# Local attention with values behind scores, and a feed-forward that reads its shifted input by copies and multiplies in three rounded passes

## The chip, the core and the metric

One NeuronCore of a Trainium2 chip runs the whole program. The metric is the device time of that one core, in microseconds (us). The kernel before was timed three times: 2302.34, 2305.26 and 2305.34 us, a median of 2305.26 us.

## What is computed

The input x has 16 batches of 128 tokens by 128 features, all float32. Four steps follow, each with a residual: a cross attention of 16 heads of 8, a mixture of 16 experts (6 per token), a cross attention of 8 heads of 64 with rotary tables, and then the part that takes most of the time, six layers of local attention and feed-forward. One of these layers is, cut to what matters:

```
shift(t): a, s = halves of the 128 features; s moves down one token (row 0 is zero)
attention:  q, k, v = shift(x) @ Wqkv             # 16 heads of 64
            q = q/|q| * q_scale, k = k/|k| * k_scale, rotary tables on both
            sim = 8 * q.k in windows of 32 tokens, each looking at itself and the one before
            x = x + softmax(sim) @ v @ Wo
feed-forward: xn = layernorm(shift(x)) * g + bln
            a, gate = halves of (xn @ W1 + b1)    # 2 x 341 columns
            x = x + (a * gelu(gate)) @ W2 + b2
```

## The kernel before

The program is written by hand for five engines, each with its own instruction stream: PE (matmuls), ACT, DVE, POOL, and SP, which only issues copies. They meet through semaphores. X and Y hold all 16 batches in on-chip memory, with the 128 tokens on the partitions. Nothing but weights and the first input comes from outside.

**Attention.** The work of a layer is cut into 64 units: 16 batches by 4 groups of four heads. Each engine runs a `Pipeline`: a list of (skew, stage). In slot c it does each stage in the order of the list, for unit c minus the skew. The first 8 slots of a layer are written out (`start`), the next 56 are a loop of 7 turns of 8 slots (`steady`, whose waits count with registers), and the last ones (slots 64 to 71, `finish(0)` to `finish(7)`) drain it.

PE's stages, in the order in which a slot issues them: scores (L854 is the mask in bfloat16, L862 the 32 small products of 64 rows by 32 columns of the array), turning q and k (L835, four transposes), values (L882, 32 small products of 64 by 32), the projection in three rounded passes of 512 columns for q and k (L818) and of 256 for v (L827), output (L902), turning the results (L892), turning the probabilities (L845) and, once in four slots, turning x (L808).

ACT squares the projection (L1194), takes the logarithm (L1200) and the guess of 1/|q| (L1205), copies v (L1187), results (L1216), probabilities (L1182) and turned q and k (L1210), and does the exponentials (L1174). DVE rotates (L1593, L1597, which free bank 0 for the next projection), sums the squares (L1607), floors them (L1622), finds the peaks (L1615), divides (L1630, L1632), splits x (L1584) and adds the residual (L1640).

POOL, in order in a slot: `l_norm` improves the guess by a Newton step in four small operations (L541, L543, L546, L548), `l_add` adds the two rotated halves (L534) and `l_scale` scales (L555). PE's turns L835 wait for L555; L534 waits for the turns two units back, since `l_qk` has two buffers.

SP moves the values of each batch to other partitions (L360, 8 copies) and fetches each batch's shifted x from Y by two copies, one of 128 rows and one of 127 (`take_x`, L367 and L368).

**Feed-forward.** A layer's 16 batches are 4 groups g of 512 tokens. For each group, `f_shift` on PE makes the shifted input in PSUM by two matmuls (L923 with the identity, L924 with a shifting matrix). DVE takes the statistics (L1653, L1658), POOL the reciprocal root `f_rs` (L566, L568) and adds b2 to Y (L571), DVE normalises into `f_n` (L1666), PE turns (L932), ACT copies with gain and bias (L1227). Then follow three chunks k of hidden columns: `f_hidden` multiplies in float32 (L948 the gate half, L949 the other), ACT does the gelu (L1235), DVE the gated product (L1676). Each chunk's two PSUM banks are free again two chunks later. `f_out` (L959) multiplies by W2 and DVE adds the residual (L1683).

The drain of a layer's attention and the feed-forward are woven together by hand in `into_feed_forward`, and the feed-forward and the next layer's first slots in `out_of_feed_forward`, where ACT and DVE also round and split the next layer's weights (L1278, L1745, `w_low`). hidden(g, k) below is the hidden product of group g and chunk k. Before, PE's order is: finish(0, 1), shift(0), finish(2, 3), turn(0), finish(4), hidden(0, 0), finish(5), shift(1), finish(6), hidden(0, 1), turn(1), hidden(0, 2), shift(2), and so on. DVE takes the statistics of group 0 after finish(1), and those of group 1 after the first gated product.

## Time and profile before

| | |
|---|---|
| median of 3 runs | 2305.26 us |
| the profiled execution | 2298.88 us, of which 2297.1 us are its span |
| PE busy | 2163.7 us (94%) |
| DVE, ACT, POOL busy | 1708.3 (74%), 1555.0 (68%), 1410.4 us (61%) |
| TensorE clock granted, mean | 0.98 of full speed |
| copies moved | 82.33 MB, 13.5% of 16 engines' span |

The profile is one execution, taken by the hardware profiler. Busy times are sums over instructions, and PE's ends are modelled, so matmuls that follow one another overlap in it. The first 540 us or so are the two cross attentions and the experts; then six layers follow. The chain of waits is followed back from the last instruction, at each step to what released it; "issue" is time in which an engine waited for nothing that the profile shows. An idle time in brackets stands ahead of the instruction, with what ended it.

### The profile page before, as it was taken

How to read it: one execution, taken by the hardware profiler on the slowest of the kernel's cores; microseconds unless marked ns; L12 is line 12 of the kernel's file. 1: busy time of each engine (PE TensorE's matmuls, PEld its weight loads, DVE VectorE, ACT ScalarE, POOL GpSimd, SP SyncE). 2: the span in 40 equal slices, each digit the busy share in tenths (PEclk: the TensorE clock that was granted, in tenths of full speed). 3: DMA queues.
4: the chain of work that ended last, by engine and by line, in shares of the span. 5: the costliest groups of instructions: out<-in, count | busy, mean ns of one | idle time of the engine just before them, and what ended most of it. 6: DMA issues, size and time to landing. Idle time of an engine off the chain costs nothing.

```text
span 2297.1 us, 104869 instructions
## 1 busy us (share of the span) xinstructions
PE 2163.7 (94%) x36357; PEld 1677.6 (73%) x36357; DVE 1708.3 (74%) x4617; ACT 1555.0 (68%) x5192; POOL 1410.4 (61%) x2639
## 2 busy tenths in 40 slices
PE   6999789998999989999899998999989999899998
PEld 4776267776888758887588875788857888578885
DVE  4777878886888758787578875778757877578874
ACT  3553545554888748887488884888848888478883
POOL 3442711112888728887288882888828888288881
PEclk9997999997999999999999999999999999999999
DMA  3000000001211102111021110311103111021110
GB/s 102 0 0 1 0 1 0 0 0 54 75 41 42 35 26 75 40 42 35 23 77 42 41 36 18 81 42 39 39 18 79 42 40 40 16 51 43 42 40 20
DMA packets 120016, 82.33 MB, mean 36 GB/s; under 512 B 50998, under 2 KB 112580, under 8 KB 119876
## 3 DMA queue, kind: packets, MB, share of 16 engines
q1 hardware_dynamic: 119876, 80.43, 13.5%
q8 instruction: 92, 1.51, 0.3%
q14 instruction: 48, 0.39, 0.1%
HBM read 21.94 MB, written 1.05 MB: 10 GB/s over the span
## 4 chain that ended last, share of the span: by engine, by line
PE 74%; issue 5%; DVE 4%; POOL 2%; ACT 1%; DVEq 0%; POOLq 0%; ACTq 0%
PE bank L818 14%; PE bank L835 9%; PE bank L902 7%; PE bank L882 6%; PE bank L862 6%; PE bank L827 6%; PE bank L892 4%; PE bank L845 4%; PE bank L757 2%; PE bank L854 2%; PE bank L746 2%; PE bank L949 2%; PE bank L948 2%; PE bank L605 2%; PE bank L959 1%
## 5 line engine op out<-in xcount | busy, mean ns | idle before, releaser
L534 POOL TENSOR_TENSOR l_qk<-l_rot 128x512 f32<-128x512 f32 x384 | 494.2, 1287 | 106.0 <-DVE l_rot L1597 58.8
L1593 DVE TENSOR_TENSOR l_rot<-bank,l_tab 128x512 f32<-128x512 f32 x384 | 265.0, 690 | 185.7 <-ACT l_sq L1194 185.1
L1210 ACT ACTIVATE l_qkT<-bank 128x512 f32<-128x512 f32 x384 | 229.6, 598 | 255.2 <-PE bank L835 255.2
L555 POOL TENSOR_TENSOR l_qk<-l_qk,l_rn 128x512 f32<-128x512 f32 x384 | 400.7, 1044 | 0.9
L1174 ACT ACTIVATE prob<-bank,peak 128x64 f32<-128x64 f32 x1536 | 353.9, 321 | 1.3 <-DVE peak L1615 1.3
L818 PE MATMUL bank<-w_high,xs_part 128*128 128x512 f32 x768 | 347.4, 452 | 6.0 <-DVE xs_part L1584 5.4
L1597 DVE TENSOR_TENSOR l_rot<-bank,l_tab 128x512 f32<-128x512 f32 x384 | 261.4, 681 | 0.0
L1607 DVE TENSOR_REDUCE l_ss<-l_sq 128x8 f32<-128x512 f32 x384 | 259.6, 676 | 0.2
L835 PE MATMUL bank<-const,l_qk 128*128 128x128 f32 x1536 | 252.9, 287 | 6.5 <-POOL l_qk L555 5.8
L1194 ACT ACTIVATE l_sq<-bank 128x512 f32<-128x512 f32 x384 | 236.0, 615 | 23.8 <-PE bank L818 16.0
L902 PE MATMUL bank<-l_wo,l_oT 128*128 128x128 f32 x1536 | 237.4, 277 | 0.0
L827 PE MATMUL bank<-w_high,xs_part 128*128 128x256 f32 x768 | 199.9, 283 | 11.6 <-issue 11.6
L902 PEld LDWEIGHTS bank<-l_wo,l_oT 128*128 128x128 f32 x1536 | 204.8, 191 | 3.3 <-issue 0.3
L835 PEld LDWEIGHTS bank<-const,l_qk 128*128 128x128 f32 x1536 | 161.9, 141 | 42.9 <-POOL l_qk L555 9.6
L818 PEld LDWEIGHTS bank<-w_high,xs_part 128*128 128x128 f32 x768 | 144.9, 189 | 63.9 <-DVE xs_part L1584 7.1
L882 PE MATMUL bank<-l_v,probT 64*32 64x65 f32 x4608 | 177.2, 223 | 10.0 <-ACT probT L1182 6.5
L439 POOL TENSOR_SCALAR ln_rs<-ln_mv 128x1 f32<-128x1 f32 (+1 forms) x64 | 14.5, 227 | 274.2 <-DVE ln_mv L1561 129.4
L1615 DVE TENSOR_REDUCE peak<-bank 128x4 f32<-128x256 f32 x384 | 160.0, 417 | 28.9 <-PE bank L862 27.3
L862 PE MATMUL bank<-l_qkT 64*32 64x64 f32 x12288 | 174.7, 222 | 0.0
L882 PEld LDWEIGHTS bank<-l_v,probT 64*32 64x32 f32 x4608 | 115.4, 106 | 79.1 <-issue 79.1
L1632 DVE TENSOR_TENSOR o<-bank,rsum 128x256 f32<-128x256 f32 x384 | 163.0, 424 | 13.3
L882 PE MATMUL bank<-stash,probT 64*32 64x65 f32 x7680 | 172.2, 223 | 0.0
(201 smaller groups left out, 5287.8 us busy)
## 6 DMA issues: line engine op xcount, KB each, us to landing
stash<-l_v SPq DMA_DIRECT2D x768, 65.0 KB, 2.0
early<-in_L_ffn_Wqkv_dram SPq DMA_DIRECT2D x36, 256.0 KB, 3.1
l_wo<-in_L_ffn_Wo_dram SPq DMA_DIRECT2D x6, 512.0 KB, 4.0
xin<-Y SPq DMA_DIRECT2D x96, 32.0 KB
xin<-Y SPq DMA_DIRECT2D x96, 31.8 KB
f_w<-in_L_ffn_W_dram SPq DMA_DIRECT2D x6, 341.0 KB
out_dram<-X SPq DMA_DIRECT2D x4, 256.0 KB, 2.3
f_w<-in_L_ffn_W_dram SPq DMA_DIRECT2D x6, 128.0 KB
```

The source lines that it names most:

```text
L534: pool.tensor_tensor(l_qk[:, k], l_rot[:, k, 0], l_rot[:, k, 1], ALU.add).then_inc(l["add_done"], 1)
L555: pool.tensor_tensor(v, v, l_rn[:, k, :, None].broadcast_to([128, 8, L_DIM]), ALU.mult).then_inc(l["qk_done"], 1)
L818: ins = pe.matmul(bank[:, 0, :].rearrange("p (q n) -> p q n", q=2), xs_part[:, part, j // 4], w[:, 0:2, 256 * g:256 * g + 256], start=n == ...
L827: ins = pe.matmul(bank[:, 1, 0:256], xs_part[:, part, j // 4], w[:, 2, 256 * g:256 * g + 256], start=n == 0, stop=n == 2)
L835: ins = pe.transpose(bank[:, 2, n * 128:(n + 1) * 128], l_qk[:, j % 2, n * 128:(n + 1) * 128], ident)
L862: ins = pe.matmul(bank[w * WINDOW:(w + 1) * WINDOW, 3 + r, BAND * p:BAND * (p + 1)], l_qkT[rows, j % 2, queries:queries + WINDOW], l_qkT[r ...
L882: ins = pe.matmul(bank[w * WINDOW:(w + 1) * WINDOW, 6 - p, at:at + L_DIM + 1], probT[rows, j % 2, 128 * r + w * WINDOW:128 * r + (w + 1) * ...
L902: ins = pe.matmul(bank[:, 7, 256:384], l_oT[:, j // 4, p], l_wo[:, p], start=p == 0, stop=p == 7, skip_group_check=True)
L1174: ins = act.activation(prob[:, k, n * BAND:(n + 1) * BAND], bank[:, 3 + r, p * BAND:(p + 1) * BAND], ACT.Exp, bias=peak[:, k, n:n + 1])
L1593: dve.tensor_tensor(l_rot[:, k, 0].rearrange("p (q h n) -> p q h n", q=2, h=4), bank[:, 0, :].rearrange("p (q h n) -> p q h n", q=2, h=4), ...
L1597: dve.tensor_tensor(l_rot[:, k, 1].rearrange("p (q h s n) -> p q h s n", q=2, h=4, s=2), bank[:, 0, :].rearrange("p (q h s n) -> p q h s n ...
L1607: dve.tensor_reduce(l_ss[:, k, :, 0], l_sq[:].rearrange("p (h n) -> p h n", n=L_DIM), AX.X, ALU.add)\
```

## The change

1. **PE's order in a slot** becomes turns L835, scores L854 and L862, values L882, and then the rest as it was.
2. **POOL's Newton step** loses one of its four operations: ACT squares the guess (a new stage of ACT, into `l_yy`), POOL multiplies that by the sum. POOL's order becomes scale, add, norm, with the norm one slot earlier. On DVE the rotation comes ahead of the residual.
3. **Copies.** `take_x` fetches the 127 shifted rows by two copies, of 112 and 15 rows.
4. **The feed-forward's input** is no longer made by PE. SP copies it from Y, four batches at a time, in three copies (128, 112 and 15 rows): groups 0 and 1 behind the moves of batch 11, group 2 behind those of batch 13, group 3 after the last. `f_n`, `f_rs` and the turned PSUM bank get two buffers, so that groups 0 and 1 are normalised within the drain: DVE has stats(0) after finish(0), stats(1) and norm(0) after finish(1), norm(1) after finish(2); POOL has rstd(0) after finish(0) and rstd(1) after finish(1). Whoever reads one of groups 0 to 2 waits for the copies of all three.
5. **The hidden products** are made in three passes of the rounded format (high by high, low by high, high by low) in place of one float32 product. ACT rounds W1 once a layer (`f_wh`) and each group's input (`f_high`); DVE subtracts to get the low parts (`f_wl`, `f_low`).
6. Semaphores are shared among the layer norms of the earlier parts.

```diff
@@ pool
+                    pool.wait_ge(l["squared"], upto(ub, u + 1))
+                    pool.tensor_tensor(t, l_s[:, k], l_yy[:, k], ALU.mult).then_inc(l["newton"], 1)
-                    pool.tensor_tensor(t, l_s[:, k], y, ALU.mult).then_inc(l["newton"], 1)
-                    pool.wait_ge(l["newton"], upto(3 * ub, 3 * u + 1))
-                    pool.tensor_tensor(t, t, y, ALU.mult).then_inc(l["newton"], 1)
...
-                return Pipeline(pool, [(4, l_norm), (3, l_add), (4, l_scale)], UNITS, UNROLL, 4)
+                return Pipeline(pool, [(4, l_scale), (3, l_add), (3, l_norm)], UNITS, UNROLL, 4)
...
             def into_feed_forward(ly, att):
+                rstd_n, bias = feed_forward(ly)
                 att.steady()
-                att.finish(0, 1, 2, 3)
+                att.finish(0)
+                rstd_n(0)
+                att.finish(1)
+                rstd_n(1)
+                att.finish(2, 3)
                 pool.wait_ge(ld_fw, (ly + 1) * (16 * FW_DMAS))
-                feed_forward(ly, 0)
+                bias(0)
@@ tensor
-                stages = [(5, l_scores), (4, l_turn_qk), (6, l_pv), (1, l_project_qk), (1, l_project_v), (7, l_output), (6, l_turn_o), (5, l_turn), (0, l_turn_x)]
+                stages = [(4, l_turn_qk), (5, l_scores), (6, l_pv), (1, l_project_qk), (1, l_project_v), (7, l_output),
+                          (6, l_turn_o), (5, l_turn), (0, l_turn_x)]
...
-                    pe.matmul(bank[0:n, at, :], f_w1[:, FF + c0:FF + c0 + n], f_nT[:, g % 2], start=True, stop=True)
-                    pe.matmul(bank[0:n, at + 1, :], f_w1[:, c0:c0 + n], f_nT[:, g % 2], start=True, stop=True)\
-                      .then_inc(f["hidden"], 1)
+                    passes = (f_wh, f_high[:, g % 2]), (f_wl, f_high[:, g % 2]), (f_wh, f_low[g % 2])
+                    for half, first in ((0, FF + c0), (1, c0)):
+                        for m, (w, x) in enumerate(passes):
+                            ins = pe.matmul(bank[0:n, at + half, :], w[:, first:first + n], x, start=m == 0,
+                                            stop=m == 2)
+                    ins.then_inc(f["hidden"], 1)
...
-                att.finish(0, 1)
-                shift(0)
-                att.finish(2, 3)
+                att.finish(0, 1, 2)
+                turn_n(0)
+                att.finish(3)
+                turn_n(1)
                 pe.wait_ge(ld_fw, (ly + 1) * (16 * FW_DMAS))
-                turn_n(0)
                 att.finish(4)
                 hidden(0, 0)
-                att.finish(5)
-                shift(1)
-                att.finish(6)
+                att.finish(5, 6)
                 hidden(0, 1)
@@ scalar
+                def l_square_guess(u, b, j):
+                    k = j % 2
+                    act.wait_ge(l["guessed"], upto(ub, u + 1))
+                    act.activation(l_yy[:, k], l_y[:, k], ACT.Square).then_inc(l["squared"], 1)
...
-                att.finish(0, 1, 2, 3)
+                att.finish(0)
                 act.wait_ge(ld_fw, (ly + 1) * (16 * FW_DMAS))
+                act.activation(f_wh, f_w1[:], ACT.Copy).then_inc(f["wh_done"], 1)
+                att.finish(1, 2)
                 copy_n(0)
+                att.finish(3)
+                copy_n(1)
@@ vector
-                att.finish(0, 1)
+                att.finish(0)
                 stats(0)
-                att.finish(2, 3)
+                att.finish(1)
+                stats(1)
                 norm(0)
+                att.finish(2)
+                norm(1)
+                dve.wait_ge(f["wh_done"], upto(0, ly + 1))
+                dve.tensor_tensor(f_wl, f_w1[:], f_wh.bitcast(F32), ALU.subtract).then_inc(f["w_split"], 1)
+                att.finish(3)
+                split(0)
                 att.finish(4, 5)
-                dve.wait_ge(ld_fw, (ly + 1) * (16 * FW_DMAS))
+                split(1)
                 gated(0, 0)
-                stats(1)
                 att.finish(6)
-                norm(1)
...
-                    if 0 < g < 3:
-                        stats(g + 1)
+                    if g < 2:
+                        stats(g + 2)
...
                     if 0 < g < 3:
-                        norm(g + 1)
+                        split(g + 1)
+                    if g < 2:
+                        norm(g + 2)
```

## Rows read from the trace of the kernel before

**Rows 1.** Two stages of one layer: stretch, busy us by engine, clock, DMA.

```profile
851.93:1082.32 230.39, 227.38 (x5131) 187.32 (x5132) 182.98 (x459) 188.24 (x692) 193.69 (x378) 1.00 0.20 51
1082.32:1140.56 58.24, 49.07 (x440) 30.70 (x438) 32.25 (x91) 25.07 (x54) 13.13 (x19) 0.97 0.05 13
```

**Rows 2.** Chain of waits in a loop slot: start us, us, what.

```profile
1284.33 0.38 PE bank L862 x32
1284.71 0.59 PE bank L835 x4
...
1285.69 0.89 PE bank L818 x3
...
1287.59 0.22 PE bank L845 x2
...
1287.92 0.38 PE bank L862 x32
```

**Rows 3.** The same chain in the feed-forward of the second layer.

```profile
1097.55 0.48 PE bank L923 x2
...
1098.62 0.90 DVE f_st L1653 x4
...
1100.55 1.05 POOL f_rs L568
...
1105.02 1.71 PE bank L949 x2
...
1112.45 0.86 PE bank L948 x2
...
1134.46 0.70 PE bank L818 x3
```

**Rows 4.** PE in order of time: start us, us, instruction [idle before].

```profile
700.59 0.21 PE L882 MATMUL bank<-l_v,probT 64*32 64x65 f32 x1
700.73 0.50 PE L818 MATMUL bank<-w_high,xs_part 128*128 128x512 f32 x1
```

**Rows 5.** POOL in order of time, one slot of the loop.

```profile
702.90 0.20 POOL L541 TENSOR_TENSOR l_t<-l_s,l_y 128x8 f32<-128x8 f32 x1
703.18 0.20 POOL L543 TENSOR_TENSOR l_t<-l_t,l_y 128x8 f32<-128x8 f32 x1
...
704.33 1.28 POOL L534 TENSOR_TENSOR l_qk<-l_rot 128x512 f32<-128x512 f32 x1 [0.28 <-PE bank L835]
705.58 1.04 POOL L555 TENSOR_TENSOR l_qk<-l_qk,l_rn 128x512 f32<-128x512 f32 x1
706.67 0.20 POOL L541 TENSOR_TENSOR l_t<-l_s,l_y 128x8 f32<-128x8 f32 x1
```

**Rows 6.** PE in order of time at the head of the loop.

```profile
1277.17 0.66 PE L835 MATMUL bank<-const,l_qk 128*128 128x128 f32 x4
1277.86 0.21 PE L882 MATMUL bank<-l_v,probT 64*32 64x65 f32 x1
```

**Rows 7.** Groups by line: ACT's guess. Busy us, mean ns, idle before.

```profile
L1205 ACT ACTIVATE l_y<-l_y 128x8 f32<-128x8 f32 x384 | 85.8, 223 | 0.2
```

**Rows 8.** DVE in order of time at the head of the loop.

```profile
1277.53 0.42 DVE L1615 TENSOR_REDUCE peak<-bank 128x4 f32<-128x256 f32 x1 [0.22 <-issue]
...
1278.67 0.42 DVE L1632 TENSOR_TENSOR o<-bank,rsum 128x256 f32<-128x256 f32 x1
```

**Rows 9.** Waits of the copy queue: us in total, times, longest.

```profile
SPq L278 <- ACT l_v L1187: 741.6, 184, 22.9
```

**Rows 10.** All engines where slot 65 of the second layer begins on PE.

```profile
1078.70 0.28 PE L854 MATMUL bank<-l_mask,cbf 128*128 128x128 bf16 x2
...
1078.91 0.68 DVE L1597 TENSOR_TENSOR l_rot<-bank,l_tab 128x512 f32<-128x512 f32 x1
```

**Rows 11.** PE in order of time in the feed-forward of the second layer.

```profile
1093.92 1.02 PE L948 MATMUL bank<-f_nT,f_w 128*128 128x512 f32 x2
...
1103.13 0.65 PE L932 MATMUL bank<-const,f_n 128*128 128x128 f32 x4 [2.50 <-DVE f_n L1666]
```

More of the change, by code:

```diff
@@ L244, in build @@
         ld_xin = [sem(f"ld_xin{k}") for k in range(2)]
+        ld_fx = [sem(f"ld_fx{k}") for k in range(2)]
         tables, scaled_q = sem("tables"), sem("scaled_q")
@@ L373, in next_x, with take_feed_forward @@
                 take_x(ly, b + 2, k)
+            def take_feed_forward(ly, first, end):
+                sp.wait_ge(l["res_done"], upto(ly * B, end))
+                apart(sp)
+                for b in range(first, end, 4):
+                    four = slice(b, b + 4)
+                    sp.dma_start(f_x[:, four, 0:HALF], Y[:, four, 0:HALF]).then_inc(ld_fx[b // 12], 16)
+                    for rows in SHIFTED:
+                        sp.dma_start(f_x[rows.start + 1:rows.stop + 1, four, HALF:], Y[rows, four, HALF:])\
+                          .then_inc(ld_fx[b // 12], 16)
             def serve_layer(ly, last):
@@ L1748, in _ @@
             first = attention(0)
+            dve.wait_ge(preset, 2)
             second.finish(0)
```

201 lines of the change are left out of this document (117 added, 84 removed).

## The prediction

> **What bounds the kernel now.** I first read the busy times by stage, then the chain of waits, then POOL's instructions in order of time. The 6 layers of local attention and feed-forward repeat every 288.6 us. One layer is 230.4 us of attention (64 units, so 3.60 us each and some extra) and 58.2 us of feed-forward, taken from POOL's last L541 of one layer to its first of the next [rows 1]. PE is busy 227 of 230 us there, but its ends are modelled, so this alone decides nothing. Attention is thus the larger lever, by 4 to 1: 0.1 us per unit is 38 us of the kernel.
>
> In attention the chain of waits lies on PE alone. One slot (one unit at each of its stages) goes from L862 at 1284.33 to L862 at 1287.92, which is 3.59 us with no idle time in it [rows 2]. Every fourth slot has L808 in it and takes 3.77, and the loop's head costs about 0.28 per 8 slots; the mean is (6 x 3.60 + 2 x 3.77 + 0.28) / 8 = 3.68 us.
>
> The reader should see a second thing in that chain. Four turns (L835) are charged 0.59 us, while two turns (L845) take 0.22, so four should take 0.44. Three passes of L818 after the tiled block L882 are charged 0.89, but 0.70 where no tiled block stands ahead of them [rows 2, 3]. So the two blocks of 32 small matmuls (L862 scores, L882 values: 64 rows by 32 columns of the array each) cost more at their borders than their neighbours need: the array waits 0.15 to 0.3 us each time it goes into and out of such a block. L882's last matmul starts at 700.59 and L818's first only at 700.73 [rows 4], where L882's own 32 follow each other within 0.25.
>
> POOL has almost no room either. From L541 at 702.90 to the next at 706.67 it takes 3.77 us, with 0.28 of it waiting for PE's L835 [rows 5], of which some 0.1 is its usual issue time: its own chain is 3.60 us too. It waits for PE only where PE takes 3.77. ACT (188 of 230 us) and DVE (183) have 20% free [rows 1]. So a slot is bound by PE and POOL together: one alone made shorter would bring next to nothing, and the change shortens both.
>
> **Part 1: order of PE's stages.** Before: mask L854, scores L862, turns L835, values L882, projection. After: turns, mask, scores, values, projection. The same instructions are issued; only one run into and out of the tiled form goes. Gone with it: the 0.15 that L835 carries over 0.44, and one exit of 0.14 (700.59 to 700.73). Upper bound: 0.28 us per slot, so PE's own chain would be 3.60 - 0.28 = 3.32.
>
> Against it stands this: the waits that the values' stage issues (for probT, o, oT and the moved values, counted with registers) now stand right behind the scores. The scores' 32 matmuls last 0.38 us; before, the turns' 0.59 covered those waits as well. At the loop's head, where registers are worked out anew, even that was not enough: L835 starts at 1277.17 and L882 only at 1277.86, 0.69 where an ordinary slot has 0.59 between them [rows 2, 6]. So issuing these waits costs several tenths; the trace has no row of L882 right behind L862 with its data ready. Ends: nothing left over (gain 0.28) and the whole gain eaten (0). I take half, 0.14 per slot, because the one place where the cover fails shows it by 0.1 only, but with the turns' 0.44 more of cover than will be left. On 56 looped slots per layer: 7.8 us.
>
> Weighed against a page: the Trainium skill, "TensorEngine Tiling (Array Packing)", section "Key Properties", says that a change of tiling mode drains the array. The 0.15 and 0.14 above agree. By that rule alone the sum would use 0.28. "TensorE: Matmul & The Clock Gate", section "Architectural detail: the array is 16× 32×32, not 1× 128×128", gives PE a queue of 64 entries; were the waits hidden by it, 0.28 would hold too. That is the first rival below.
>
> **Part 2: POOL's Newton step.** y squared moves to ACT (384 more ACT operations like L1205, 0.22 us each [rows 7]), and L543 goes. L541 to L543 is 0.28 of POOL per unit [rows 5]. POOL's chain becomes 3.32. So POOL stays below PE's 3.46, and its gain is worth only what lets PE's gain through. The loops over several engines are the next thing that is late. One runs over DVE: 0.6 from the scores to the peaks, 1.56 from the peaks (1277.53) to the end of o (1279.09) [rows 8], 0.15 to L892, then 0.22 + 0.22 + 0.44 + 0.2 on PE back to the scores [rows 2]: 3.4 us, near PE's 3.46 but not above. ACT's new operation lies in its free 20%.
>
> **Part 3: the static slots** (first 8 of a layer) are POOL's at 3.35 each; they gain up to 0.28, and I take 1 us per layer. The copies of 112 and 15 rows are one more issue per batch on SP, which waits 742 us for ACT's values [rows 9], and a batch has 14 us; the 12 copies of the feed-forward's input stand there too, eight slots ahead of their reader. Nothing; if they land late, it is the statistics below that wait.
>
> **Part 4: into the feed-forward.** Per layer, the shifts go from PE (two matmuls, the first 0.48 on the chain, 4 x 0.9 us in all), and the fp32 hidden products of 2 x 0.86 become two runs of three passes like L818's, 2 x 0.70 [rows 3]: 12 x 0.33 = 4.0 us. That is 7.6 us of PE work. It doesn't come out whole, since the stages are linked anew.
>
> DVE's statistics of group 0 now stand behind its slot 64, and POOL's f_rs of group 0 stands between POOL's slots 64 and 65. POOL runs about a slot ahead: until now it had finished its slot 65 before DVE's last L1597 (from 1078.91, 0.6 in pitch); PE's slot 65 began at 1078.70 [rows 10]. After the change POOL waits for the statistics, and L555 of slot 65, which PE's turns want, comes behind. Counted from PE's slot 65: DVE is free at 0.8, statistics and f_rs take 3.0 (1098.62 to 1101.60 [rows 3]), L555 1.1 [rows 5]: the turns start at 4.9 in place of 0. The same again for group 1, behind DVE's own slot 65: 3.4 us. On the way the ends of the slots gain little, and ACT's copies (f_high four times and f_wh once a layer) stand ahead of probT. I get the first hidden product at 22.6 after PE's slot 65, against 15.2 before (1093.92 [rows 11]): **7.4 us later**.
>
> Given back: PE's wait of 2.5 us for f_n of group 1 (up to 1103.13 [rows 11]) goes, with the slow clock behind it (L949 1.71 in place of 0.86 [rows 3]), and the shifts; but f_n of group 2 now stands behind DVE's last residual (2.0 us of idle PE). The second hidden product of group 1 comes at 36.0, against 33.7 before (1112.45 [rows 3]). For groups 1 and 2 PE's work is 14.1 us where it was 18.3, but DVE becomes the bound: in group 1 it has statistics 1.35, f_n 1.3, the new f_low 0.6, three gated products 2.1, the residual 0.6 and three w_low pieces 1.8, 7.8 us together, against PE's 7.3. I get the next layer's first projection 1.5 us early, and 0.5 more from the shorter hidden products behind it: 2.0 us. Two stalls of over 3 us on PE should bring the slow clock back once or twice (one stretch costs about 1.7 us now, half of it in that L949): minus 1.5. **Net 0.5 us per layer**, with ends from +4 (the stalls covered) to -5.
>
> **Sum**, against the profiled execution's 2298.9 us: 6 x (7.8 + 1.0 + 0.5) = 56 us, so 2243. The three runs' median is 6.4 above the profiled one (2305.3 against 2298.9), so **2249 us**.
>
> **Rivals.**
> (a) The border's whole 0.28 comes out, because PE has the waits issued in time. PE and POOL are then both at 3.32: 6 x (15.7 + 1 + 0.5) = 103 us, 2202. For it: the page on tiling and the 0.15 and 0.14; against: [rows 6]. Chance 0.2.
> (b) **Slower.** Half of it is that the waits behind the scores eat the border's gain (0 per unit); the mechanism that decides is the one above, POOL held in its slots 65 and 66 by DVE's statistics. If the 8 us of stalls are not given back, because DVE in group 1 stays behind, a layer loses 5 us: 2305 + 30 = 2335. It decides from the point where the gain per unit is under 0.09 us. For it: PE's own waits on POOL here are real; against: 2.5 us and the slow clock are sure to go. Chance 0.12.
> (c) The passes or the order don't do what they are meant to (no gain in attention, feed-forward even): 2300 to 2305. Chance 0.08.
> (d) The forecast, 2225 to 2275: 0.6.
>
> The range for 8 in 10 reaches into (a) and over (c)'s near end: 2200 to 2292. What a measurement of this kernel can tell from no change is about 0.2%, 4.6 us. Faster by more: (a), (d) and part of (c), 0.82; within: 0.06; slower: 0.12.
>
> **What would show it.** Period of POOL's L541 in the loop: 3.68 now; 3.53 by (d), 3.40 by (a), 3.68 by (c). PE: the gap from L862's last to L882's first, about 0.1 to 0.4 by (d), near nothing by (a); L835 at 0.44. POOL: a wait at f_rs of about 4 us in each of its slots 64 and 65, with PE idle at L835 there; if that is missing, part 4 is wrong. Hidden products at 0.23 per pass, or the term of 4.0 falls. DVE without idle time in the feed-forward's group 1. A slow clock in those slots and none at hidden(0,2).

## The result and the profile after

The changed kernel took 2327.13 us (median of 4 runs, 2324.91 to 2328.2), the kernel before 2303.8 us beside it: a ratio of 1.0107, with a 95% interval of 1.0089 to 1.0124. It is slower, by 1.1%. The forecast was 2249 us with a range that ended at 2292.

The profiled execution has a span of 2326.4 us. The stretches are those of [rows 1], cut at POOL's first and last Newton step of the second layer (L589 in the new file): core 0, busy us by engine, clock, DMA.

```profile
858.41:1096.63 238.22, 225.90 (x5146) 194.54 (x5152) 188.44 (x479) 197.45 (x757) 183.81 (x319) 0.98 0.21 53
1096.63:1149.89 53.26, 41.88 (x445) 32.47 (x443) 34.59 (x76) 27.14 (x58) 10.44 (x14) 0.98 0.08 20
```

The attention stage grew from 230.4 to 238.2 us and the rest shrank from 58.2 to 53.3. PE has less to do in both (225.9 for 227.4, and 41.9 for 49.1 us), so the time is idle time. To see where it lies, I cut a layer at three instructions of PE instead, its turns of units 0, 4 and 60 (L835 before, L896 after). The means are of the last five layers for the first two columns and of the first five for the third; the first layer's start is left out, being overlapped with the cross attention.

| kernel | ratio to before | slot, turns of unit 4 to 60 (56 slots) | start, unit 0 to 4 | drain and feed-forward, unit 60 to the next layer's unit 0 |
|---|---|---|---|---|
| before | 1 | 3.689 us | 13.7 us | 68.8 us |
| after | 1.0107 | 3.665 | 12.8 | 75.7 |

Each ratio below is to runs of the kernel before on the same chip. By layer the loop gained 56 x 0.024 = 1.3 us, the start 0.9, and the drain with the feed-forward lost 6.9. That is 4.7 us per layer, 28 in all; the profiled executions differ by 29.

**The loop.** This is the chain of waits on PE in the third layer, as [rows 2]: start us, us, what. L896 are the turns, L923 the scores, L943 the values, L879 the projection.

```profile
1281.07 0.44 PE bank L896 x4
...
1281.61 0.39 PE bank L923 x32
1282.00 0.41 PE bank L943 x24
1282.40 0.90 PE bank L879 x3
...
1284.62 0.65 PE bank L896 x4
...
1285.38 0.39 PE bank L923 x32
1285.77 0.20 issue
1285.97 0.46 PE bank L943 x29
...
1288.71 0.60 PE bank L896 x4
```

The first slot shown takes 3.55 us (1281.07 to 1284.62), the second, at the loop's head, 4.09. The turns are at 0.44 us, as forecast. Between scores and values the second slot has 0.20 us that is charged to nothing but issue. By the starts on PE (medians of the last five layers), scores to values take 0.32 to 0.42 us in six slots of eight, and 0.65 and 0.55 in the other two.

**The drain.** POOL in order of time, from its slot 64 of the second layer on (start us, us, instruction, idle before and what ended it). L594 ends the Newton step, L613 and L615 are `f_rs`, L601 scales what PE turns.

```profile
1080.84 0.20 POOL L594 TENSOR_TENSOR l_rn<-l_t,l_y 128x8 f32<-128x8 f32 x1
1085.33 0.23 POOL L613 TENSOR_SCALAR f_rs<-f_mv 128x4 f32<-128x4 f32 x1 [4.29 <-DVE f_mv L1724]
1085.64 1.04 POOL L615 TENSOR_TENSOR f_rs<-f_rs,minus_half 128x4 f32<-128x4 f32 x1
1086.65 1.04 POOL L601 TENSOR_TENSOR l_qk<-l_qk,l_rn 128x512 f32<-128x512 f32 x1
...
1092.93 0.38 POOL L613 TENSOR_SCALAR f_rs<-f_mv 128x4 f32<-128x4 f32 x1 [3.19 <-DVE f_mv L1724]
```

And PE in the same stretch, with two later waits for the values:

```profile
1082.70 0.38 PE L906 MATMUL bank<-const,prob 128*128 128x128 f32 x2
1087.74 0.69 PE L896 MATMUL bank<-const,l_qk 128*128 128x128 f32 x2 [4.67 <-POOL l_qk L601]
...
1095.51 0.85 PE L896 MATMUL bank<-const,l_qk 128*128 128x128 f32 x4 [2.96 <-POOL l_qk L601]
...
1102.23 0.21 PE L943 MATMUL bank<-l_v,probT 64*32 64x65 f32 x1 [1.32 <-ACT probT L1234]
...
1106.92 0.21 PE L943 MATMUL bank<-l_v,probT 64*32 64x65 f32 x1 [1.67 <-ACT probT L1234]
```

POOL waits for DVE's statistics between its slots 64 and 65 and again behind 65; PE stands for 4.67 and 2.96 us at its turns. Then PE waits 1.32 and 1.67 us for `probT`, which ACT copies behind the feed-forward's input. ACT in order of time:

```profile
1100.10 0.78 ACT L1285 ACTIVATE f_nT<-bank,f_g 128x512 f32<-128x512 f32 x1 [1.44 <-PE bank L984]
1100.91 0.63 ACT L1288 ACTIVATE f_high<-f_nT 128x512 fp32r<-128x512 f32 x1
1101.45 0.36 ACT L1273 ACTIVATE l_oT<-bank 128x256 f32<-128x256 f32 x1
1101.71 0.37 ACT L1234 ACTIVATE probT<-bank 128x256 f32<-128x256 f32 x1
```

The theory that I took to the chip from this, called **A**: the loop gains next to nothing, since PE's waits in front of the values take back the 0.14 us; and the stalls of the drain come from POOL's place for `f_rs`, and nothing behind them has the room to give them back. The rivals stand with each run.

### The profile page after: what moved, and what is told of

The parts are those of the page before. It is cut to its first block, busy times and chain, and to the rows that moved or that the text cites. A ratio compares the mean times of both kernels' runs of the same rounds, so it can differ in the third digit from the quotient of the medians.

```text
span 2326.4 us, 104822 instructions
## 1 busy us (share of the span) xinstructions
PE 2123.5 (91%) x36405; PEld 1743.1 (75%) x36405; DVE 1752.7 (75%) x4647; ACT 1621.9 (70%) x5606; POOL 1335.5 (57%) x2256
## 4 chain that ended last, share of the span: by engine, by line
PE 74%; issue 5%; DVE 4%; ACT 2%; POOL 1%; DVEq 0%; DMA 0%; SPq 0%; POOLq 0%; ACTq 0%
PE bank L879 14%; PE bank L896 8%; PE bank L963 7%; PE bank L943 7%; PE bank L923 6%; PE bank L888 6%; PE bank L953 4%; PE bank L906 4%; PE bank L1004 3%; PE bank L1015 2%; PE bank L818 2%; PE bank L915 2%; PE bank L807 2%; PE bank L666 2%; PE bank L786 1%
## 5 line engine op out<-in xcount | busy, mean ns | idle before, releaser
L601 POOL TENSOR_TENSOR l_qk<-l_qk,l_rn 128x512 f32<-128x512 f32 x384 | 400.7, 1044 | 60.2 <-POOL l_rn L594 12.1
L879 PE MATMUL bank<-w_high,xs_part 128*128 128x512 f32 x768 | 343.4, 447 | 6.7 <-DVE xs_part L1649 5.3
L896 PE MATMUL bank<-const,l_qk 128*128 128x128 f32 x1536 | 241.2, 281 | 51.9 <-POOL l_qk L601 48.9
L1246 ACT ACTIVATE l_sq<-bank 128x512 f32<-128x512 f32 x384 | 233.8, 609 | 22.9 <-PE bank L879 12.8
L963 PE MATMUL bank<-l_wo,l_oT 128*128 128x128 f32 x1536 | 243.6, 282 | 2.8 <-ACT l_oT L1273 2.8
L896 PEld LDWEIGHTS bank<-const,l_qk 128*128 128x128 f32 x1536 | 178.4, 143 | 69.6 <-POOL l_qk L601 52.9
L943 PE MATMUL bank<-l_v,probT 64*32 64x65 f32 x4608 | 198.6, 226 | 30.2 <-ACT probT L1234 17.9
L888 PE MATMUL bank<-w_high,xs_part 128*128 128x256 f32 x768 | 199.9, 282 | 11.5 <-issue 11.5
L879 PEld LDWEIGHTS bank<-w_high,xs_part 128*128 128x128 f32 x768 | 144.3, 188 | 64.3 <-issue 9.7
L943 PE MATMUL bank<-stash,probT 64*32 64x65 f32 x7680 | 188.9, 228 | 0.0
L943 PEld LDWEIGHTS bank<-l_v,probT 64*32 64x32 f32 x4608 | 145.6, 106 | 52.9 <-issue 45.7
L923 PE MATMUL bank<-l_qkT 64*32 64x64 f32 x12288 | 177.5, 225 | 0.0
```

What stands on the lines that cost most here:

```text
L601: pool.tensor_tensor(v, v, l_rn[:, k, :, None].broadcast_to([128, 8, L_DIM]), ALU.mult).then_inc(l["qk_done"], 1)
L879: ins = pe.matmul(bank[:, 0, :].rearrange("p (q n) -> p q n", q=2), xs_part[:, part, j // 4], w[:, 0:2, 256 * g:256 * g + 256], start=n == ...
L888: ins = pe.matmul(bank[:, 1, 0:256], xs_part[:, part, j // 4], w[:, 2, 256 * g:256 * g + 256], start=n == 0, stop=n == 2)
L896: ins = pe.transpose(bank[:, 2, n * 128:(n + 1) * 128], l_qk[:, j % 2, n * 128:(n + 1) * 128], ident)
L923: ins = pe.matmul(bank[w * WINDOW:(w + 1) * WINDOW, 3 + r, BAND * p:BAND * (p + 1)], l_qkT[rows, j % 2, queries:queries + WINDOW], l_qkT[r ...
L943: ins = pe.matmul(bank[w * WINDOW:(w + 1) * WINDOW, 6 - p, at:at + L_DIM + 1], probT[rows, j % 2, 128 * r + w * WINDOW:128 * r + (w + 1) * ...
```

## Which part brings what

Four kernels: before with parts 1 and 2 (b_att), with part 1 alone (b_order), with part 2 alone (b_newton), and the changed kernel with the hidden products as one float32 product again (a_fp32).

```diff
 b_att, b_order
-                stages = [(5, l_scores), (4, l_turn_qk), (6, l_pv), ...
+                stages = [(4, l_turn_qk), (5, l_scores), (6, l_pv), ...
 b_att, b_newton
-                return Pipeline(pool, [(4, l_norm), (3, l_add), (4, l_scale)], ...
+                return Pipeline(pool, [(4, l_scale), (3, l_add), (3, l_norm)], ...
 a_fp32
-                    passes = (f_wh, f_high[:, g % 2]), (f_wl, f_high[:, g % 2]), (f_wh, f_low[g % 2])
+                        ins = pe.matmul(bank[0:n, at + half, :], f_w1[:, first:first + n], f_nT[:, g % 2],
+                                        start=True, stop=True)
```

> The kernel before with parts 1 and 2 alone: PE's order turns, scores, values, and the Newton step with one POOL operation less (POOL, ACT and DVE orders as in the change); the feed-forward and its input stay as before. Theory A (the loop gains almost nothing, since an ordinary slot gets 0.14 us shorter but PE's waits in front of the values take it back in two or three slots of eight; the loss sits in the drain): slot mean 3.66 to 3.67 as in the changed kernel, against 3.68; 6 x 48 x 0.02 = 6 us gained, 2298 us (2292 to 2304). Rival B (the two parts are worth what I forecast, 0.14 per unit, and something that the new feed-forward input brings, such as its copies, slows the loop): 2303.8 - 47 = 2257 us. Rival C (the attention parts are themselves the loss): over 2310.

> The kernel before with part 1 alone (PE's order), POOL keeping its four Newton operations. Theory A: POOL's own chain of 3.60 us holds the slot, so that nothing of the 0.14 us comes out of an ordinary slot, and the waits in front of the values cost something on top: slot mean 3.68 to 3.75, 2304 to 2325 us. Rival B (POOL has room after all, since its issue times shrink when it isn't kept waiting): slot mean 3.55, 2265 us. PE's turns at 0.44 us in both.

> The kernel before with part 2 alone (POOL's Newton step one operation shorter, POOL's order scale, add, norm, ACT's square, DVE's rotation ahead of the residual); PE's order as before. Theory A (PE alone sets the slot as soon as POOL has room, and POOL's four operations only just kept up before): the slot stays at 3.68 or 3.69, since PE's own chain holds it, and the start of each layer gains what POOL's static slots gain, 0.5 to 1 us; ratio to before 0.998 (0.996 to 1.000). Rival J (the slot in the kernel before was set by POOL in part): slot 3.65, 0.992. With this run b_order's slot of 3.74 and b_att's of 3.67 are the four corners: by theory A part 1 is worth +0.05 alone and -0.02 behind part 2.

> The changed kernel with the hidden products as one float32 product again (no rounded copies on ACT, no low parts on DVE); all else as changed. Theory A (PE has waits in this stretch, but is the bound from group 2 on; the passes save 0.29 us per product pair there, 12 x 0.29 = 3.5 us, of which ACT's and DVE's extra work in the drain eats part): 0 to 3 us slower per layer, 2327 to 2345 us, likeliest 2336. Rival E (the passes are the loss, because ACT's roundings stand ahead of probT and DVE's subtractions ahead of the peaks): 2 us per layer faster, 2315 us.

| kernel | parts | ratio to before (95%) | slot | start | drain and feed-forward |
|---|---|---|---|---|---|
| b_order | 1 | 1.0108 (1.009 to 1.0126) | 3.742 | 14.0 | 69.7 |
| b_newton | 2 | 0.9979 (0.9965 to 0.9992) | 3.678 | 13.7 | 69.2 |
| b_att | 1, 2 | 0.9946 (0.9926 to 0.9966) | 3.669 | 12.9 | 69.0 |
| a_fp32 | 1 to 4, 6 | 1.0152 (1.0133 to 1.017) | 3.664 | 12.9 | 77.8 |
| after | all | 1.0107 (1.0089 to 1.0124) | 3.665 | 12.8 | 75.7 |

By the slots, the four corners of parts 1 and 2 are as theory A has them. Part 1 alone lengthens the slot by 0.05 us and makes the kernel 1.1% slower. PE asks for POOL's result 0.6 us earlier than before, while POOL still has its four operations. The waits of b_order in the loop of one layer (1190 to 1360 us) print it, in total us, times and longest:

```profile
PEld bank L835 <- POOL l_qk L555: 2.2, 11, 0.2
```

PEld is PE's weight load. The same list has no such row for before, b_att or the changed kernel, and the 46 slots of this stretch lose 46 x 0.053 = 2.4 us. Part 2 alone is worth 0.01 us per slot, since PE holds the slot. Its ratio is within what was expected of it, but the 0.5 to 1 us expected at the start of each layer did not come: 13.7 us, as before. Together the two parts are worth 0.02 us per slot. b_att came out faster than expected (0.9946 against 0.9975) mostly by what I had left out: the start of each layer is 0.8 us shorter, as in the changed kernel. Neither part alone shortens it (14.0 and 13.7 against 13.7). Rivals B and C of b_att fall: the attention parts are worth 0.5%, neither the 2% of the forecast nor a loss.

Part 5 is a gain: without it the kernel is 0.45% slower (1.0152 against 1.0107), 2.1 us per layer. Rival E falls. So the loss is in part 4: from b_att to a_fp32, which adds parts 3 and 4 (and 6, ahead of the layers), the drain and feed-forward grow by 8.9 us per layer, while slot and start stay. Part 3 was not run alone; that it isn't the loss follows from a_rstd1 below, which has it and gives 6.7 us back.

## Where the loop's gain went

b_waits moves PE's waits ahead: the one for the copied values by one slot, behind the projections, those for the bank's readers to between turns and mask. b_dose adds four semaphore increments between scores and values, b_dose_out the same four ahead of the output products. b_att_moved moves the wait for the copied values alone.

```diff
 b_dose, in l_pv
-                    apart(pe)
+                    for _ in range(5):
+                        apart(pe)
 b_dose_out, in l_output
+                    for _ in range(4):
+                        apart(pe)
 b_waits; b_att_moved without l_read
-                    results_read(l_pv, b, j % 4)
-                    if j % 2 == 0:
-                        pe.wait_ge(moved[j // 4][j % 4 // 2], (ly * B + b - j // 4) * 32 + 64)
...
+                stages = [(4, l_turn_qk), (6, l_read), (5, l_scores), (6, l_pv), (1, l_project_qk), (1, l_project_v),
+                          (5, l_moved), (7, l_output),
```

> b_att with four more semaphore increments issued by PE right in front of the values' products, between scores and values; they move no data and nobody waits for them. Theory A (what PE's sequencer has to work through between scores and values is paid in full, as the array is idle there): each costs its 0.05 to 0.13 us in every unit, 0.2 to 0.5 us per slot, 70 to 170 us in all, ratio 1.03 to 1.07. Rival K (the sequencer is ahead of the array, so that a few instructions cost nothing): 0.995.

> b_att with the same four increments in front of the output products, behind 1.15 us of projections of six long passes. Theory A' (there the sequencer is ahead of the array and the increments are hidden): within 0.3% of b_att, ratio 0.993 to 0.998. Rival G (an instruction of the sequencer costs the same wherever it stands): the same as b_dose.

> The kernel before with parts 1 and 2 (as in b_att) and two of PE's waits moved: the one for the copied values one slot ahead, behind the projections, and the ones for the bank's readers between the turns and the mask; what stands between the scores and the values is the wait for probT alone. Theory A (what takes back the border's gain is that PE's sequencer works through these waits while the array stands idle between scores and values, 0.65 and 0.54 us in two slots of eight against 0.32 to 0.35 in the others): these two fall to 0.35, 0.5 us per eight slots = 0.06 per slot, slot mean 3.60 in place of 3.67; 336 x 0.06 = 20 us under b_att, a ratio to before of 0.986 (0.982 to 0.990). Rival F (the wait in these slots is for data, probT or the copied values, and only stands there): no change, 0.9946. Rival G (the waits cost the same wherever they stand): 0.9946 or more, with the gap now at the mask.

> b_att with the wait for the copied values (every second unit, with a register to be worked out) moved from in front of the values to behind the projections one slot before; the waits for the bank's readers stay. Theory A' (a wait there is covered as the four increments of b_dose_out were): the gaps of 0.65 and 0.54 us between scores and values fall by 0.1 to 0.25, the slot mean from 3.67 to 3.63 or 3.64, ratio 0.990 (0.988 to 0.993). Rival G' (the register work is what costs, and it is paid at either place): 0.9946 or more.

| kernel | ratio to before (95%) | slot |
|---|---|---|
| b_att | 0.9946 (0.9926 to 0.9966) | 3.669 us |
| b_dose | 1.0755 (1.0737 to 1.0772) | 4.161 |
| b_dose_out | 0.9939 (0.9922 to 0.9955) | 3.677 |
| b_waits | 1.0019 (1.001 to 1.0029) | 3.715 |
| b_att_moved | 0.9932 (0.9915 to 0.9949) | 3.653 |

Four increments between scores and values cost (4.161 - 3.669) / 4 = 0.12 us each, the same four ahead of the output 0.002 us each. The chains of waits of these two show it (L861 scores; L882 values in b_dose, L881 in b_dose_out). First b_dose:

```profile
1246.63 0.38 PE bank L861 x32
1247.01 0.56 issue
1247.58 0.46 PE bank L882 x29
```

And b_dose_out, two slots with the output L903 between them:

```profile
1247.55 0.38 PE bank L861 x32
1247.93 0.13 issue
1248.06 0.46 PE bank L881 x29
...
1249.79 0.45 PE bank L903 x4
...
1251.21 0.39 PE bank L861 x32
1251.60 0.41 PE bank L881 x20
```

So theory A of b_dose stands, and rival K falls: what PE's sequencer has to work through behind the scores is paid in full, and ahead of the output it is free. The scores are 64 instructions (a weight load and a product for each of 32 blocks) in 0.38 us. That the sequencer has no lead behind these, and has one behind six long projection passes, is how I read the two runs.

Moving the real waits did not bring what was expected. b_waits was to gain 20 us on b_att and is 0.7% slower. Its gap between scores and values fell to 0.27 us in every slot, but the values behind it rose to 0.52, the turns to 0.60 in three of eight slots and the output to 0.50 to 0.66 in several. That is rival G: the readers' waits, put between turns and mask, are paid there too, and theory A of b_waits falls. b_att_moved leaves these where they were. Its two long gaps fell from 0.65 and 0.55 to 0.41 and 0.31, and the slot by 0.016 us. With that the two blocks are back at 0.8 us in both slots, 0.4 us less in eight, but the output behind the loop's head rose from 0.44 to 0.64, and only 0.13 us of the 0.4 is left. The kernel is 0.14% faster than b_att, within both intervals: half or less of what A' expected, and by the ratio alone it can't be told from nothing. So these runs place part of the time that the new order loses, behind the scores, and none of them gives it back.

One more thing is to be read in these rows. The two blocks of 32 take 0.27 + 0.52 = 0.79 us in b_waits, 0.32 + 0.48 in b_att_moved, and 0.385 + 0.392 in the kernel before, where the turns stand between them. Side by side they are not shorter than apart. What the new order saves is the 0.15 us that the turns carried behind the scores (0.59 to 0.44); the 0.14 that I had added for a second exit did not come out in any of these kernels. By the Trainium skill, "TensorEngine Tiling (Array Packing)", section "Key Properties", a change of tiling mode drains the array; here one of the two borders taken away had a price, and the other one none.

## Where the drain's time went

All start from the changed kernel. a_rstd1 puts each of POOL's first two `f_rs` one slot later. a_copies adds to it that ACT's copies for the feed-forward stand behind those of o, probT and the turned operands. a_stats2 adds to a_rstd1 that group 2 is normalised in the drain as well.

```diff
 a_rstd1, POOL
-                att.finish(0)
-                rstd_n(0)
-                att.finish(1)
-                rstd_n(1)
-                att.finish(2, 3)
+                att.finish(0, 1)
+                rstd_n(0)
+                att.finish(2)
+                rstd_n(1)
+                att.finish(3)
 a_copies, ACT (part: the stages 0 to 7 or 8 to 9 of a slot)
-                copy_n(0)
-                att.finish(3)
-                copy_n(1)
-                att.finish(4, 5)
+                att.part(3, 0, 8)
+                copy_n(0)
+                att.part(3, 8, 10)
+                att.part(4, 0, 8)
+                copy_n(1)
+                att.part(4, 8, 10)
+                att.finish(5)
 a_stats2, DVE (POOL's rstd_n(2) behind bias(0))
                 norm(1)
+                stats(2)
...
                 gated(0, 0)
+                norm(2)
```

> The changed kernel with POOL's rstd of groups 0 and 1 each one slot later in the drain (behind its slots 65 and 66 in place of 64 and 65); nothing else differs. Theory A (POOL waiting for DVE's statistics holds PE for 4.7 and 3.0 us per layer, and no later stage had slack for it): the two waits of 4.29 and 3.19 us on POOL fall under 1 us each, PE's two stalls at its turns go, the last eight slots of a layer take 27 in place of 34.2 us, and 5 to 7 us per layer come back: 2327 - 6 x 6 = 2291 us (2285 to 2300). Rival D (behind the stalls something else is late anyway: the normalised input of groups 0 and 1 on DVE and ACT, so that the time is only moved): under 2 us per layer, 2315 to 2327.

> a_rstd1 with ACT's copies of the normalised input of groups 0 and 1 taken from the head of its slots 67 and 68 to just before the exponentials of these slots, so that they stand behind the copies of o, of probT and of the turned scores' operands. Theory A (after the POOL waits, the drain is held by ACT's 1.4 us of copies ahead of probT: PE waits 1.3 and 1.7 us for probT there): these two waits go, 1 to 2.5 us per layer, a ratio to before of 0.989 in place of 0.9938 (0.9875 to 0.992). Rival H (the input of the feed-forward is then what comes late, and the first hidden product waits the same time): within 0.5 us per layer, 0.9925 to 0.995.

> a_rstd1 with the statistics, the rstd and the normalising of group 2 moved ahead into the drain (DVE: statistics behind norm(1), normalising behind gated(0,0); POOL: behind its first bias), where POOL now waits 15.8 us for them. Theory A (in each layer PE reaches turn(2) 6.7 us after hidden(0,1) begins, where its own work there is 3.0 and the jump of the layer loop 2.5): f_n of group 2 is the late one; with it early 1 to 2 us per layer come out, ratio to before 0.990 (0.987 to 0.992). Rival I (the jump back of the loop, 2.5 us on PE, and DVE's gated products behind it are the bound): under 0.5 us per layer, 0.993 to 0.995.

> All of these together on the changed kernel: rstd later, ACT's copies later, group 2 early, PE's waits moved. Theory A: the sum, 20 + 10 + 8 us under a_rstd1, about 0.978 of before (0.972 to 0.984), 2248 us where before takes 2299. If the parts of the drain hide each other, 0.985.

| kernel | ratio to before (95%) | slot | drain and feed-forward |
|---|---|---|---|
| after | 1.0107 (1.0089 to 1.0124) | 3.665 | 75.7 us |
| a_rstd1 | 0.9938 (0.992 to 0.9956) | 3.665 | 69.0 |
| a_copies | 0.9849 (0.9832 to 0.9865) | 3.664 | 65.2 |
| a_stats2 | 0.9955 (0.9939 to 0.9972) | 3.665 | 69.4 |
| a_all | 0.9973 (0.9963 to 0.9983) | 3.717 | 66.7 |

Two lines of POOL's order turn 1.1% slower into 0.6% faster: 6.7 us per layer come back, within theory A's 5 to 7, and rival D falls. POOL in a_rstd1 has no wait at `f_rs` any more:

```profile
1079.22 0.23 POOL L613 TENSOR_SCALAR f_rs<-f_mv 128x4 f32<-128x4 f32 x1
1079.53 1.04 POOL L615 TENSOR_TENSOR f_rs<-f_rs,minus_half 128x4 f32<-128x4 f32 x1
1080.54 1.04 POOL L601 TENSOR_TENSOR l_qk<-l_qk,l_rn 128x512 f32<-128x512 f32 x1
```

PE's waits from there to the next layer, in total us, times and longest, lead on. In a_rstd1:

```profile
PE bank L943 <- ACT probT L1234: 2.6, 2, 1.7
PE bank L953 <- DVE o L1697: 2.4, 5, 1.3
PE bank L1004 <- issue: 2.3, 1, 2.3
```

The 2.6 us for probT are the next to go, and in the same list of a_copies there is no row for probT. That brought 3.8 us per layer, above what was expected (1 to 2.5): the first hidden product begins 1.8 us earlier (20.5 us behind the turns of unit 60 in place of 22.3), and the rest comes out behind it. It is more than the 2.6 us of waits, all the more since PE's waits for `o` rose from 2.4 to 4.1 us in the same list. What differs besides is TensorE's granted clock. In a_rstd1 it is 0.66 in 1075 to 1080 us, 0.69 in 1090 to 1095 and 0.83 in 1100 to 1120, in a_copies 1.00 in 1068 to 1098, 0.83 in 1098 to 1108 and 1.00 from there. That the clock is the rest of the gain fits, but no run tests it. Rival H falls.

Group 2 moved ahead (a_stats2) brought nothing, 0.17% slower than a_rstd1 with intervals that overlap. Theory A's 0.990 falls; rival I (0.993 to 0.995) is the nearest. PE's waits in a_stats2 say where it went:

```profile
PE bank L953 <- DVE o L1697: 4.2, 4, 1.8
PE bank L1004 <- DVE f_h L1747: 2.5, 2, 1.9
```

With DVE's extra work in the drain, `o` and `f_h` are late by as much as was saved. a_all, which has all three and b_waits' move, is no sum and misses both of its expectations (0.978 and 0.985): 66.7 us in the last column, more than a_copies alone, and b_waits' longer slot on top.

Two smaller runs. a_bias holds POOL's first addition to Y back until group 1 is normalised. a_best moves the normalising of group 1 one slot later, with its turning and copies. a_best_moved has b_att_moved's edit as well.

```diff
 a_bias, POOL
+                pool.wait_ge(f["n_done"], upto(0, ly * 4 + 2))
                 bias(0)
 a_best, DVE
                 att.finish(2)
-                norm(1)
...
                 att.finish(3)
+                norm(1)
```

> a_copies with POOL's first addition to Y of the feed-forward (128x512, 1.27 us) held back until the input of group 1 is normalised. Theory A (DVE's four normalising operations took 1.09 us where POOL was idle and 1.89 and 2.80 us where POOL had 128x512 operations at the same time, because the two engines hold each other up): norm(1) takes about 2.0 us in place of 2.80, DVE's peaks of slot 67 come 0.8 us earlier, and 0.3 to 0.8 us per layer come out: ratio to before 0.984 (0.982 to 0.9855), where a_copies has 0.9849. Rival L (the length of these four has another cause, such as f_n's place): norm(1) stays at 2.80 us and the time too.

> a_copies with the normalising of group 1 one slot later on DVE (behind its slot 67, where POOL has nothing left to run), its turning on PE behind slot 68 and its copies on ACT behind slot 69. Theory A (norm(1), stretched to 2.8 us by POOL's operations, stands ahead of DVE's peaks of slot 67 and holds scores, exponentials and values behind it): norm(1) takes about 1.1 us and the peaks come 2 us earlier; 1 to 2 us per layer, ratio 0.981 (0.979 to 0.983) where a_copies has 0.9849. Rival M (then the first hidden product waits for split(0) behind norm(1), and the time is the same): 0.984 to 0.986.

> a_best and b_att_moved's move together. Theory A and A': 0.976 to 0.979. By the rivals M and G': 0.984 to 0.986.

DVE's four normalising operations of group 1 in a_copies, a_bias and a_best, each from its own order of time:

```profile
1080.18 2.80 DVE L1740 TENSOR_SCALAR c_oT<-m_xT,f_mv,f_rs 128x128 f32<-128x128 f32 x4 [0.48 <-POOL f_rs L620]
```

```profile
1075.34 1.83 DVE L1741 TENSOR_SCALAR c_oT<-m_xT,f_mv,f_rs 128x128 f32<-128x128 f32 x4
```

```profile
1081.20 1.11 DVE L1738 TENSOR_SCALAR c_oT<-m_xT,f_mv,f_rs 128x128 f32<-128x128 f32 x4
```

In a_copies POOL has two large operations in this stretch:

```profile
1080.12 1.04 POOL L606 TENSOR_TENSOR l_qk<-l_qk,l_rn 128x512 f32<-128x512 f32 x1
1081.12 1.27 POOL L625 TENSOR_TENSOR Y<-Y,f_b 128x512 f32<-128x512 f32 x1
```

So 2.80 us beside two of POOL's, 1.83 beside one, 1.11 beside none: theory A of a_bias, and rival L falls. The kernel's time hardly noticed: 0.9843 (0.9827 to 0.986) and 0.9851 (0.9835 to 0.9868) against a_copies' 0.9849. In a_best the peaks behind it wait 2.2 us for PE's scores instead, so it is rival M that stands: DVE's norm(1) is not what ends the drain. a_best_moved is at 0.9847 (0.9831 to 0.9864): the 0.014 us that its slot gains (3.648 against 3.662) are 5 us on 336 slots, and its drain and feed-forward lose 0.5 us per layer again. What holds the drain at 65 us was not settled.

**a_copies beats both kernels**: 2266.33 us, 1.5% under before, 2.6% under the changed kernel.

## Why the prediction was wrong, point by point

The forecast was 2243 us for the profiled execution, whose own time is 2328: 85 us, or 14 per layer. Two terms of the sum failed. The loop's was to be 7.8 us per layer and was 1.3, 6.5 too much; the feed-forward's was to be plus 0.5 and was minus 6.9, 7.4 too much.

**Part 1, the bound.** I took 0.28 us as what two borders cost, and half of it. Of the 0.28 only the 0.15 of the turns was there. The "one exit of 0.14 (700.59 to 700.73)" is still there: by their starts the two blocks take 0.39 + 0.39 us before, apart, and 0.79 after, side by side. The 0.14 per slot that I forecast does come out of the best slots, three of eight, which take 3.47 to 3.49 us for 3.60, by the starts of L879.

**Part 1, what stands against it.** I had named it (the waits of the values right behind the scores, several tenths to issue) and then priced it from [rows 6] at half of the gain. The 0.02 us per slot that are left are 0.15 in eight slots, where eight times 0.13 should have come out. Of the 0.9 us missing, 0.4 lie there: in two slots of eight the two blocks take 0.94 and 1.04 us for 0.79. The loop's head and the two slots behind it take 4.04, 3.81 and 3.70 us where they took 3.92, 3.75 and 3.60 (means of the last five layers). The other half is spread over values of 0.56 us in one slot, output products of 0.49 for 0.44 in two, and the turns of x (L869, 0.27 for 0.15) and of the probabilities at the head; what PE stands for there stays open. I put no price on a waiting instruction. b_dose gives one, 0.12 us for a semaphore increment. Rival (a), the whole 0.28 at a chance of 0.2, counted an exit that no kernel here gives back. The Trainium skill, "TensorE: Matmul & The Clock Gate", section "Architectural detail: the array is 16× 32×32, not 1× 128×128", names a queue of 64 entries, which I took as a reason for (a). b_dose_out shows such a lead behind long passes; b_dose shows none behind 64 short instructions.

**Part 2.** POOL's chain did become shorter and does let PE's gain through: b_order and b_att differ by 0.07 us per slot. Part 3's 1 us per layer came (0.9), but not as forecast: I had the static slots down as POOL's alone, and part 2 alone leaves them at 13.7 us (b_newton). That the number is right is luck.

**Part 4, the stalls.** Forecast 4.9 and 3.4 us at the turns of PE's slots 65 and 66; measured 4.67 and 2.96. The step that read them from the order of POOL's and DVE's programs was right, and so was the clock: in 1080 to 1100 us, with the two stalls in it, the granted clock fell to 0.78 and 0.71. That is between its two levels of 1.2 and 2.4 GHz, as a mean of a stretch that has both.

**Part 4, the first hidden product.** Forecast 7.4 us late, measured 10.7: 25.9 us after PE's slot 65 where it was 15.2 (11.5 in the mean of five layers, counted from the turns of unit 60). The waits of 1.32 and 1.67 us for probT are 3.0 us that were missing. I had listed ACT's copies ahead of probT and charged them nothing of their own, and a_copies, which moves them, has neither wait. The slow clock of the stalls, which I had set against the gains further on, falls into this stretch too.

**Part 4, what is given back.** From the first hidden product to the next layer's first turns the forecast had the changed kernel 7.9 us faster. It is 5.8 us faster in this layer and 4.6 in the mean of five. In this layer, up to the second hidden product of group 1 I had 5.1 us and 3.3 came; from there to the next layer's first projection 3.8, and 1.9 came; behind that minus 1.0, and plus 0.6 came. I had named DVE as the bound of this stretch, and DVE it is (6.97 of 7 us busy in 1125 to 1132). The size of one term was wrong: I priced `f_n`, DVE's four normalising operations, at 1.3 us, as they were. Before, they read the shifted input from PSUM (`bank`), where `f_shift` left it; since part 4 they read SP's copy in SBUF (`m_xT`). Group 2 before, then groups 2 and 3 after, with POOL's addition to Y beside them:

```profile
1112.36 1.26 POOL L571 TENSOR_TENSOR Y<-Y,f_b 128x512 f32<-128x512 f32 x1
1112.51 1.37 DVE L1666 TENSOR_SCALAR f_n<-bank,f_mv,f_rs 128x128 f32<-128x128 f32 x4 [1.03 <-POOL f_rs L568]
...
1117.15 1.98 DVE L1732 TENSOR_SCALAR f_n<-m_xT,f_mv,f_rs 128x128 f32<-128x128 f32 x4 [1.67 <-POOL f_rs L615]
...
1124.63 2.98 DVE L1732 TENSOR_SCALAR c_oT<-m_xT,f_mv,f_rs 128x128 f32<-128x128 f32 x4 [0.26 <-POOL f_rs L615]
```

From PSUM they take 1.36 us with POOL idle and 1.37 beside POOL's 1.26 us. From SBUF they take 1.10 alone (the last group of the sixth layer), 1.98 beside one addition and 2.98 beside two. That is 0.7 us for group 2, whose wait on PE was forecast at 2.0 us and is 2.66 to 2.8, and 1.7 us for group 3, so that DVE's work in group 1, forecast at 7.8 us, takes 9.7 (1121.57 to 1131.3). PE waits 0.69 us for it (L984; 0.66 before) and 0.60 for `f_h` behind it (L1004; none before). That these four operations get longer beside POOL is shown (a_bias and a_best above); how much of what was not given back comes from it was not tested by a run.

At the place of the wait of 2.5 us for `f_n` of group 1 [rows 11], which went, PE now stands for the jump back of the loop over the layers. PE in order of time, first in the first layer, which does not jump there, then in the second:

```profile
822.71 0.39 PE L1004 MATMUL bank<-f_high,f_wh 128*85 128x512 f32 x1
...
826.92 1.11 PE L984 MATMUL bank<-const,f_n 128*128 128x128 f32 x4 [2.66 <-DVE f_n L1732]
...
1114.39 0.39 PE L1004 MATMUL bank<-f_low,f_wh 128*128 128x512 f32 x1
1117.12 0.46 PE L1004 MATMUL bank<-f_high,f_wh 128*85 128x512 f32 x1 [2.34 <-issue]
...
1119.19 0.66 PE L984 MATMUL bank<-const,f_n 128*128 128x128 f32 x4 [0.44 <-DVE f_n L1732]
```

The gap of 2.15 to 2.34 us is there in the four layers that end with the jump and in neither of the two that don't. It costs next to nothing here: without the jump PE waits 2.66 us for group 2, with it 2.34 + 0.44 = 2.78 for both. The layer without it isn't faster either, since behind its 2.66 us the granted clock is 0.50 (827 to 830 us), where it stays at 1.00 in the second layer (1112 to 1125). So by these rows the jump adds 0.1 us at most to what was missing; the late input of group 2 would fill its place. The Trainium skill, "Runtime: NRT & Kernel Launch", section "Instruction fetch mechanics", says that a taken branch can force a fetch of its target before the engine goes on; the trace agrees, with these 2.15 to 2.34 us.

**The rivals.** (b) is what happened, at the chance of 0.12: almost nothing left of the border's gain (0.02 of 0.14), DVE behind in group 1, and a layer that loses more than the 5 us it had (6.9); its 2335 was 8 us from the measured time. I had both of its mechanisms, and the stalls to 0.5 us. The mistake was in the weighing: I let terms that are argued (given back later, half of the border) cancel stalls that were read from the programs' order.

**Part 5.** The passes run at 0.23 us. Forecast 4.0 us of PE work less per layer; 2.1 came out (a_fp32). Behind the first hidden product it is 3.3 us, but this product comes 1.2 us later than in a_fp32 (30.0 us behind the turns of unit 60 for 28.8), where ACT and DVE round and split in the drain.

## What to carry to other kernels

An engine that is made to wait for another in the middle of a pipeline's drain stalls everyone downstream by the full wait: look first where the waited-for result is made, and place the reader one slot behind it. Two lines of order were worth 1.7% here, more than all the arithmetic taken out. When an operation gets its input from another memory, price it anew, together with what runs beside it. When a wait is removed, ask what will be waited for at that place next, and price each semaphore instruction behind a block of very short matmuls at its full cost. A gain "given back later" is a forecast of its own and should not be set against a stall that the program's order makes sure.

## What the runs showed of the hardware

- A semaphore instruction of PE costs 0.12 us between two blocks of small tiled matmuls and nothing (0.002 us) behind long passes, ahead of the output (b_dose, b_dose_out).
- In the layer ahead of the layer loop, whose counts are constants, the slot is 3.60 us, in the others 3.66 (after; 3.65 and 3.69 before). That PE pays here for its registers is argued, not tested.
- Two blocks of 32 small products (64 rows by 32 columns of the array) take 0.79 us side by side and 0.78 apart.
- DVE's `TENSOR_SCALAR` of 128x128 float32 from SBUF, four times, takes 1.11 us alone, 1.83 beside one and 2.80 beside two large operations of POOL (a_best, a_bias, a_copies). From PSUM it takes 1.36 us alone and 1.37 beside one (before). The Trainium skill, "SBUF — State Buffer", section "SBUF: two separate sides", tells of a port pair in SBUF that one of the two engines holds for a whole instruction while the other is blocked, where DVE's instruction is in a two-port mode or has two inputs in SBUF; the durations agree in kind, with 0.7 us more beside 1.0 us of POOL and 1.7 more beside 2.3.
- The jump back of the layer loop keeps PE for 2.15 to 2.34 us (after). Before, PE's wait for `f_n` at that place is 2.50 us with the jump and 2.51 and 2.42 without it, so that the jump doesn't show.
